# Moving the last tiles' row transfers of a graph kernel from GpSimd to the queues of SyncE and ScalarE

## The reference: what is computed

```
dst, src = edge_index                       # receivers, senders (the graph's names)
edge_feat = concat([h[dst], h[src], rel_pos, distance], axis=-1)
x = silu(edge_feat @ W1 + b1)
x = silu(x @ W2 + b2)
scores = (x @ W3 + b3)[:, 0]
mx = segment_max(scores, dst)
exp_scores = exp(scores - mx[dst])
alpha = exp_scores / (segment_sum(exp_scores, dst)[dst] + EPS)
msg = h[src] @ Wv * (alpha * node_weight[src])[:, None]
out = layernorm(h + (h + segment_sum(msg, dst)))
```

## Time and profile before

| what | value |
|---|---|
| median of 3 runs | 991.55 us (990.44 to 994.18) |
| the profiled execution's own time | 992.99 us |
| its span | 990.9 us |
| granted clock of TensorE, mean over the span | 0.829 |

### The profile page before, as it was taken

The page is one execution under the profiler, slowest core; times in us unless marked ns, Lnnn a source line. Parts: engine busy times, 40 slices in busy tenths (PEclk is TensorE's granted clock), DMA queues, the critical chain, the costliest instruction groups (busy, mean ns, idle before and its releaser), DMA issues.

```text
span 990.9 us, 13294 instructions
## 1 busy us (share of the span) xinstructions
PE 571.3 (58%) x2587; PEld 395.2 (40%) x2587; DVE 573.3 (58%) x2275; ACT 521.9 (53%) x1168; POOL 747.0 (75%) x784
## 2 busy tenths in 40 slices
PE   0989999989803646577667766767898610000000
PEld 0657666666501323354445544545576510000000
DVE  7987877763452546598789887972577830400000
ACT  1356664545522766678699879983587460000000
POOL 6777777777777777777777777777777777777776
PEclk9999999999998877879798888887899865555555
DMA  6799999989994876888878778763443212211111
GB/s 208 230 308 331 341 322 312 306 252 311 338 219 148 275 257 231 296 279 276 287 269 300 269 250 302 270 185 93 120 121 88 76 56 68 68 53 56 55 54 48
DMA packets 87225, 206.27 MB, mean 208 GB/s; under 512 B 21253, under 2 KB 58790, under 8 KB 74600
## 3 DMA queue, kind: packets, MB, share of 16 engines
q1 hardware_dynamic: 58376, 141.17, 41.6%
q0 software_dynamic: 28096, 64.09, 22.4%
q10 hardware_dynamic: 672, 0.17, 0.1%
HBM read 113.16 MB, written 92.31 MB: 207 GB/s over the span
## 4 chain that ended last, share of the span: by engine, by line
POOL 49%; issue 23%; ACT 12%; PE 12%; DVE 4%; DMA 1%; POOLq 0%; ACTq 0%; DVEq 0%
POOL hk L459 26%; POOL out_rows L463 18%; ACT xin L515 6%; POOL region L459 4%; PE bank L669 3%; PE bank L685 3%; ACT hk L567 2%; PE bank L692 2%; PE bank L671 1%; PE bank L663 1%; DVE dst L946 1%; ACT hkT L538 1%; PE bank L656 1%; ACT L553 1%; ACT x L548 1%
## 5 line engine op out<-in xcount | busy, mean ns | idle before, releaser
L515 ACT ACTIVATE xin<-xin,drs 128x128 f32<-128x128 f32 x637 | 258.1, 485 | 39.3 <-DVE drs L931 39.2
L459 POOL DMA_INDIRECT hk<-in_xw,snd_t x196 | 188.7, 963 | 62.0 <-issue 59.4
L459 POOL DMA_INDIRECT region<-rec_d,id_t x196 | 186.6, 952 | 61.2 <-issue 57.6
L459 POOL DMA_INDIRECT hk<-in_x,kg_t x196 | 186.8, 953 | 59.7 <-issue 59.7
L463 POOL DMA_INDIRECT out_rows<-hk,sidx_t x190 | 182.8, 962 | 58.0 <-issue 57.7
L946 DVE BATCH_NORM_STATS2 dst<-xin 128x6 f32<-128x256 f32 x392 | 137.1, 415 | 56.3 <-DMA xin<-in_x 55.7
L624 PE MATMUL bank<-w1b,region 128*128 128x128 f32 x392 | 148.6, 483 | 12.6 <-DMA region<-ef_d 6.9
L669 PE MATMUL bank<-hkT,w1a 128*128 128x512 f32 x98 | 69.6, 799 | 148.7 <-issue 97.6
L624 PEld LDWEIGHTS bank<-w1b,region 128*128 128x128 f32 x392 | 99.9, 315 | 31.3 <-issue 7.3
L669 PEld LDWEIGHTS bank<-hkT,w1a 128*128 128x128 f32 x98 | 19.2, 231 | 185.1 <-issue 163.8
L548 ACT ACTIVATE x<-bank,bcol 128x512 f32<-128x512 f32 x49 | 33.4, 683 | 98.7 <-PE bank L671 98.7
(11 more groups left out here) (176 smaller groups left out, 873.2 us busy)
## 6 DMA issues: line engine op xcount, KB each, us to landing
xin<-in_x SPq DMA_DIRECT2D x49, 1024.0 KB, 7.9
out_rows<-xin SPq DMA_DIRECT2D x49, 1024.0 KB, 5.1
rec_d<-hk SPq DMA_DIRECT2D x49, 514.0 KB, 6.6
out_rows<-hk SPq DMA_DIRECT2D x432, 0.5 KB
krow<-seg_d SPq DMA_DIRECT2D x49, 128.0 KB, 3.4
out_rows<-hk ACTq DMA_DIRECT2D x336, 0.5 KB
hk<-in_xw,snd_t POOLq DMA_INDIRECT x196, 4.7
hk<-in_x,kg_t POOLq DMA_INDIRECT x196, 3.6
```

What stands on the lines that cost most here:

```text
L459: pool.indirect_dma_start(out=to, out_offset=None, in_=frm, in_offset=bass.IndirectOffsetOnAxis(ap=index, axis=0)).then_inc(done, 16)
L515: ins = nc.scalar.activation(xin[:, j % X_RING, n, :], xin[:, j % X_RING, n, :], ACT.Identity, bias=drs[:, j % 2, 1, n:n + 1], scale=drs[: ...
```

## The change

The last of the 196 tiles (40 real edges) leaves GpSimd in all four passes: its senders (one row a turn from turn 4, in the first stage), receivers (one row a step), records (20 rows in each of two steps from step 47) and finished rows (before the other finished rows at the end) are moved by SyncE, one row per DMA. Two more sender tiles of the last group are fetched by ScalarE, six rows a turn from turn 4, 256 rows in all. The last group has a ring slot of its own (a thirteenth), and GpSimd doesn't wait for a write before it. Closing rows 128 to 195 (68) are written by ScalarE, row by row, ahead of its remaining finished rows; GpSimd scatters only the first 128. A closing row with nothing to mend goes to a spare row of the output. In return only four tiles of finished rows are written row by row, not six: 320 rows by SyncE, 192 by ScalarE. VectorE clears one tile at the start and makes the list of closing row numbers with one more instruction. TensorE waits for the new transfers too. The core of the diff:

```diff
+LAST = E - (T - 1) * P
+READ, HS_FROM, REC_ROWS, REC_STEP = 8, 4, 20, G - R_RING + 10
+ACT_TILES, ACT_ROW_STEP = 2, 6
-ROW_TILES, SP_ROWS = 6, 432
+ROW_TILES, SP_ROWS = 4, 320
+FIX_ROWS, FIX_READ = T - P, 17
...
+        def moved(g):
+            return TPG if g < G - 1 else TPG - 1
+
+        def senders_moved(g):
+            return TPG if g < G - 1 else TPG - 1 - ACT_TILES
...
         def tiles_scattered(g):
-            return [q for q in range(TPG) if g * TPG + q >= ROW_TILES]
+            return [q for q in range(moved(g)) if g * TPG + q >= ROW_TILES]
...
+            def sender_rows():
+                for first in range(0, LAST, READ):
+                    for p, r in numbers(snd_last, first, READ, N - 1):
+                        sp.dma_start(rec[p:p + 1, HS_RING, TPG - 1, H:RW], xw[bass.ds(r, 1), :]).then_inc(S["hs_rows"], 16)
+                        yield
+
+            def receiver_rows():
+                sp.wait_ge(S["last_out"], 48)
...
+            def record_rows():
+                sp.wait_ge(S["z_ready"], G - R_RING)
+                for first in range(0, LAST, REC_ROWS):
+                    for p, r in numbers(last_d[0:1, :], first, REC_ROWS, EP - 1):
+                        sp.dma_start(rr[p:p + 1, (G - 1) % R_RING, TPG - 1, :], rec_d[bass.ds(r, 1), :]).then_inc(S["r_rows"], 16)
+                        yield
+
+            def last_rows():
+                sp.wait_ge(S["res_ready"], G)
...
                 dense(i)
+                if i >= HS_FROM:
+                    next(senders, None)
...
+            for k, frm in enumerate((id_t, kg_t, sidx_t)):
+                sp.dma_start(last_d[k:k + 1, :].rearrange("o p -> p o"), frm[0:LAST, T - 1:T]).then_inc(S["last_out"], 16)
...
                 dense(B0 + s)
+                if s >= 1:
+                    next(receivers, None)
+                if s >= REC_STEP:
+                    for _ in range(REC_ROWS):
+                        next(records, None)
...
+            last_rows()
             for _ in finished:
                 pass
...
-                    wait_ring(pool, rec_out, g - HS_RING, 16)
-                    for q in range(TPG):
+                    if g < G - 1:
+                        wait_ring(pool, rec_out, g - HS_RING, 16)
+                    for q in range(senders_moved(g)):
...
-                    for q in range(TPG):
+                    for q in range(moved(g)):
                         t = g * TPG + q
                         gather(hk[:, g, q, :], x, kg_t[:, t:t + 1], hk_in[g % HK_SEMS])
...
-                    for q in range(TPG):
+                    for q in range(moved(g)):
                         t = g * TPG + q
                         gather(rr[:, g % R_RING, q, :], rec_d, id_t[:, t:t + 1], r_in[g % R_RING])
...
-            for k in range(2):
-                scatter_some(yfix[:, k, :], fixi[:, k:k + 1], S["fix_out"])
+            scatter_some(yfix[:, 0, :], fixi[:], S["fix_out"])
...
+            def sender_rows():
+                for first in range(0, ACT_TILES * P, READ):
+                    _, rows = nc.values_load_multi_w_load_instructions(
+                        snd_act[0:1, first:first + READ], [mybir.EngineType.Activation], min_val=0, max_val=N - 1,
+                        skip_runtime_bounds_check_because="senders are rows of x")
+                    for n, r in enumerate(rows, first):
+                        q, p = TPG - 1 - ACT_TILES + n // P, n % P
+                        act.dma_start(rec[p:p + 1, HS_RING, q, H:RW], xw[bass.ds(r, 1), :]).then_inc(S["hs_more"], 16)
+                        yield
...
                 norm(i, 6, ACT_ROWS)
+                if i >= HS_FROM:
+                    for _ in range(ACT_ROW_STEP):
+                        next(senders, None)
...
             ins.then_inc(S["fix_res"], 1)
+            act.wait_ge(S["fix_res"], 1)
+            for first in range(0, FIX_ROWS, FIX_READ):
+                _, rows = nc.values_load_multi_w_load_instructions(
+                    fixn_d[0:1, P + first:P + first + FIX_READ], [mybir.EngineType.Activation], min_val=0, max_val=NOUT - 1,
+                    skip_runtime_bounds_check_because="receivers, or the number of a spare row where there is nothing to mend")
+                for p, r in enumerate(rows, first):
+                    act.dma_start(out[bass.ds(r, 1), :], yfix[p:p + 1, 1, :]).then_inc(S["fix_rows"], 16)
             for _ in finished:
                 pass
...
+                    if i == G - 1:
+                        pe.wait_ge(S["hs_rows"], 16 * LAST)
+                        pe.wait_ge(S["hs_more"], 16 * P * ACT_TILES)
```

More of the change, by code:

```diff
@@ L26 @@
 LASTROW = N - BN
-NOUT = N + 1 + EP
+NOUT = N + 1 + EP + T
 HS_RING, EF_RING, R_RING, X_RING = 12, 4, 12, 4
@@ L237, in gnn_kernel @@
         yrow = late(4 * H).rearrange("p (k h) -> p k h", k=4)
-        fixf = late(2)
+        fixf = late(1)
         bank = [ctx.enter_context(nc.psum_tensor(f"bank{n}", [P, GE], F32)) for n in range(8)]
@@ L275, in blocks, with slot, wait_tiles @@
             return [j for j in range(NB) if DSTEP[j] == u]
+        def slot(g):
+            return g % HS_RING if g < G - 1 else HS_RING
+        def moved(g):
+            return TPG if g < G - 1 else TPG - 1
+        def senders_moved(g):
+            return TPG if g < G - 1 else TPG - 1 - ACT_TILES
+        def wait_tiles(eng, ring, g, tiles):
+            n = len(ring)
+            eng.wait_ge(ring[g % n], 16 * sum(tiles(h) for h in range(g % n, g + 1, n)))
         def rows_of(j):
@@ L382, in load_far, with numbers @@
                 sp.dma_start(cont[0:n, b % FAR_RING, :], bass.AP(tensor=cont_d.tensor, offset=o, ap=[[P, n], [1, P]])).then_inc(to, 16)
+            def numbers(frm, first, n, top):
+                _, rows = nc.values_load_multi_w_load_instructions(
+                    frm[0:1, first:first + n], [mybir.EngineType.SP], min_val=0, max_val=top,
+                    skip_runtime_bounds_check_because="the numbers are of rows of the tensor, those of the last edges")
+                return enumerate(rows, first)
+            def sender_rows():
[5 more added lines that the diff above has]
+                sp.wait_ge(S["last_out"], 48)
+                for first in range(0, LAST, READ):
+                    for p, r in numbers(last_d[1:2, :], first, READ, N - 1):
+                        sp.dma_start(hk[p:p + 1, G - 1, TPG - 1, :], x[bass.ds(r, 1), :]).then_inc(S["hk_rows"], 16)
+                        yield
[7 more added lines that the diff above has]
+                sp.wait_ge(S["res_ready"], G)
+                for first in range(0, LAST, READ):
+                    for p, r in numbers(last_d[2:3, :], first, READ, NOUT - 1):
+                        sp.dma_start(out[bass.ds(r, 1), :], hk[p:p + 1, G - 1, TPG - 1, :]).then_inc(S["sp_rows"], 16)
+            senders = sender_rows()
             for i in range(B0):
@@ L413, in _ @@
             finished = store_rows(sp, mybir.EngineType.SP, 0, SP_ROWS, "sp_rows")
+            receivers, records = receiver_rows(), record_rows()
             for s in range(LAST_STEP):
@@ L432, in _ @@
             sp.dma_start(fara, fara_d.to_broadcast((P, T))).then_inc(S["fix_in"], 16)
-            for k, (first, n) in enumerate(((0, P), (P, T - P))):
-                sp.dma_start(fixf[0:n, k:k + 1], fixi_d[0:1, first:first + n].rearrange("o t -> t o")).then_inc(S["fix_in"], 16)
+            sp.dma_start(fixf, fixi_d[0:1, 0:P].rearrange("o t -> t o")).then_inc(S["fix_in"], 16)
             sp.wait_ge(S["parts_ready"], 1)
@@ L1131, in row_signs @@
         s = [np.where((np.arange(P) >> m) & 1, -1.0, 1.0) for m in range(7)] + [np.ones(P)]
-        return np.stack([s[0]] + [s[m - 1] * s[m] for m in range(1, 8)], 1).astype(np.float32)
+        spare = [N + 1 + EP + 2 * np.arange(P) + k for k in range(2)]
+        return np.stack([s[0]] + [s[m - 1] * s[m] for m in range(1, 8)] + spare, 1).astype(np.float32)
     arrays = {
```

55 lines of the change are left out of this document (34 added, 21 removed).

## The result

The changed kernel takes 1011.46 us (median of 4 runs, 1009.0 to 1011.84) against 992.78 us for the kernel before (4 runs, 990.44 to 994.18): a ratio of 1.0184, 95% interval 1.016 to 1.0208. It is slower by 18.7 us, where 985.2 was forecast. The profiled execution's span went from 990.9 to 1009.2 us, 18.3 more.

The account below looks back on a forecast made before the run. GpSimd's never-resting queue was taken as the bound: -3.80 senders, -1.26 receiver, -1.26 record, +1.27 scatters, -1.29 closing scatter = -6.34 us, so 991.55 - 6.3 = 985.2 us; range 983.4 to 992.0.

Parts of the forecast that it names:

- GpSimd's saving: On GpSimd's queue: 775 instructions in place of 780, 6.34 us less, taken through whole to the end of the span.
- Rival B: TensorE's last ten steps stay bound by ScalarE and VectorE: up to 5.06 us lost, centre 988.5 us; chance 0.13.
- ScalarE's price in stage one: ScalarE's queue from turn 4 on: sender rows and loads take 3.8 us a turn, 5 us late, hidden under 20 us.
- The load term: ScalarE, stage one: three quarters of a 2.01 us load of numbers per turn, 1.5 us.
- The row term: ScalarE, stage one: six sender rows a turn at 0.38 us each, 2.3 us.
- Both signs of being wrong: Wrong if GpSimd stands for a record write, or line 525's pace in turns 4 to 46 is over 5.5 us.
- How far the queue runs ahead: ScalarE, stage one: at least three activations stand ready behind a load; that least depth gives 26 us late, all 14 none.
- The cover of 20 us: First record gather: GpSimd arrives at 297.6 us, the last record write lands at about 277, so 20 us of delay hide.
- Rival A: ScalarE's queue bounds stage one in turns 4 to 46: 20 to 76 us late, middle 35, giving 1000 us; chance 0.16.
- the 30 us of cover: First receiver gather, at 251.43 us: the tables it needs are there at about 217, 30 us before.
- The 25 us of cover of the ring of sender slots: Stage one: a sender gather needs the write twelve groups earlier, which was to land 25 us before it.
- Rival C: A row queue still ends last, needing rows at 0.7 us, not 0.51: about 991 us, between 988 and 996; chance 0.05.

Follow-up runs that it names:

- the kernel that writes first and reads 16: The changed kernel with ScalarE's sender numbers read 16 at a time from a DRAM tensor, last record write ahead of SyncE's dense transfers: 984.03 us, ratio 0.991.
- the kernel with one tile: The changed kernel with one sender tile on ScalarE in place of two, three rows a turn: 985.26 us, ratio 0.9926.

## Why the prediction was wrong, point by point

**GpSimd's saving: right.** 775 instructions at the same durations. Where nothing waits (the kernel that writes first and reads 16), the span is 982.9, 8.0 under before: 6.3 for the five and about 1.3 of idle time before the last record groups, which the range had as its lower end. Rival B, TensorE's tail staying where it was, did not happen: the first scatter moved from 745.7 to 738.0 in that kernel.

**ScalarE's price in stage one: wrong, and this is the step that failed.** The prediction gave the moved sender rows 3.8 us of queue work a turn and 5 us of delay, which was to hide; the work was (91.8 us of loads)/43 = 2.1 for loads and, with about 0.15 us between them, 6 x (0.33 + 0.15) = 2.9 for rows, 5.0. The load term was 1.5, taken from a load of 16 numbers from the kernel's own `list_d`; a read of eight numbers from the input tensor cost 2.87 us in two loads, the pointer and the numbers, where 2.01 was taken, and the pointer load is in no row of before. With the same rows and fewer or shorter loads GpSimd's wait fell from 25.3 to 5 us, so it is this term that carries most of it. The row term was 2.3, taken from the end of the kernel, where the DMA engines are nearly idle. Both signs of being wrong that the prediction named came: GpSimd stood for a record write, and the turns took 5.80 us.

**How far the queue runs ahead: the bound was right, the value hidden in it mattered less.** At least three was read, eleven was true. The Trainium skill gives 8 ("Advanced Engine Details and Errata", section Engine Queue Depths). The trace of the kernel after shows eleven unstarted activations ahead of a row, and the measurement decides; what the page counts as the queue it doesn't say. With the whole turn hidden the sum by the prediction's own form is 6.3 + 2 x (0.3 + 5.0) = 16.9 per cycle, 1.8 over 15.1, 26 us late in 14.3 cycles; 36.6 were measured, of which 4.2 are there without ScalarE's rows, so that some 6 us stay unexplained. The least reading of the rows put the loss into the long turns; it is in the short ones, which have hardly any arithmetic to hide queue work.

**The cover of 20 us: wrong by nearly a half.** The last write was taken to land in 7 us. That row is of the writes before it: the view has no landing for the last one, which already stood behind two dense transfers in the kernel before:

```profile
269.27 0.35 SPq L335 DMA_DIRECT2D out_rows<-xin  x1
269.67 0.43 SPq L327 DMA_DIRECT2D xin<-in_x  x1
```

In the trace of before the last landing mark of its semaphore (15 of this write's 16 are there) comes 18.0 us after its issue, and GpSimd didn't wait for it only because it arrived later still. With the 17.4 us of the kernel after, the cover was 299.2 - (270.1 + 17.4) = 11.7. Then 36.6 - 11.7 = 24.9 us of wait, and 25.0 is what the trace shows. Both mistakes carry the wait: in the traces 13 us of it remain with the order alone mended, 5 with ScalarE's loads alone reduced, none with both.

**The range and the chances.** Rival A is what happened, by its mechanism, place and nearly its price: it had loads of 3 us and rows of 0.45, 5.0 us of queue work a turn, and 49 to 76 us late. Its middle of 35 us late was nearly the 36.6 measured; that the time is 1011 and not its 1000 is the cover, 11.7 us and not 20. Its chance of 0.16 was too low: the forecast's own costs of a load and of a row had been read where the DMA engines are nearly idle. The range ended at 992 because it left this case out.

**The rest.** VectorE's tables were late with TensorE (their last instruction at 246.8, before at 217.6), and GpSimd's first receiver gather needed them at 249.1: in time, but the 30 us of cover were down to 2. The 25 us of cover of the ring of sender slots went the same way: at 5.80 us a turn GpSimd waited twice for a slot, 1.6 us. SyncE's 40 record rows delayed the end of the steps by the 10 to 15 us that were expected: in the kernel with one tile the closing rows start at 879 us, 12 later than ScalarE's last rows. ScalarE's queue ended at 977 there, not at 951, and only 4 us ahead of GpSimd:

```profile
879.02 48.05 ACTq L676 DMA_DIRECT2D out_rows<-xin  x68
929.31 47.86 ACTq L325 DMA_DIRECT2D out_rows<-hk  x96
```

68 rows in 48.05 us are 0.71 each, for which 0.51 was taken; the 7.2 us loads are the difference. Rival C was nearer than its 0.05.

## What to carry to other kernels

A queue that issues DMAs beside its engine's arithmetic has a budget per turn, some 4 us here, and it is spent in the turns that have no arithmetic to hide it; work under that budget cost nothing and work over it slowed the stage, so price a moved step with everything it needs (the load of its address, the pointer before it) and at the load of the place that it moves to, not of the place where the trace happens to show it. When a cover is counted up to the landing of one transfer, look at what stands before that transfer on its queue: here two lines in the other order were worth 10 to 12 us. When a part is left out to price it, see in the trace that the rest is still there. And spread a small change before giving it up: half the rows, or the same rows with fewer loads and the write in front, turned 1.8% slower into 0.7 to 0.9% faster.

## What the runs showed of the hardware

- A read of an input tensor into registers is two loads in series, the pointer (1.3 us median) and the numbers (1.1 for eight); from a tensor of the kernel it is one, 1.4 us (median) for eight numbers and 2.4 for sixteen in the first stage, where the DMA engines are full, and 1.1 to 1.4 and 2.0 later on.
- Three loads of 17 numbers, from numbers 145, 162 and 179 on, took 7.2 us each, the one from number 128 on 2.4, and loads of 16 from multiples of 16 on 1.9 to 2.1.
- Single loads of 6.6 to 9.4 us came in the first stage of each kernel with sender rows on ScalarE; the runs don't tell why.
- ScalarE's queue ran a DMA while eleven earlier activations had not started.
- GpSimd could use a 0.5 MB write 5.5 us after its issue when it went ahead of 2 MB on its queue, and after 17.4 us when it stood behind them.
